# Negated scores, elu's negative part on ScalarE, and another order on VectorE in a graph attention kernel

## Chip, cores and metric

One core of a Trainium2 chip runs the whole program. The metric is device time in microseconds (us). The engines are TensorE (PE in the profile; PEld for its weight loads), VectorE (DVE), ScalarE (ACT), GpSimd (POOL) and SyncE (SP, which only issues DMAs here). Each engine runs its own instructions in order and waits on semaphores for the others.

## The reference

The input is x, 8 graphs of 1024 nodes with 256 features, and an integer adjacency matrix for each. A first attention layer is followed by three more, each with a feed-forward network, and by normalisations. The change touches the first layer only:

```python
h = jnp.einsum('bni,oi->bno', x, W) + b
ha = jnp.einsum('bmi,ij->bmj', h, attn)
scores = jnp.einsum('bmj,bnj->bmn', ha, h)
scores = jnp.where(adjacency_matrix == 0, -jnp.inf, scores)
attn_weights = jax.nn.softmax(scores, axis=-1)
x_out = jnp.einsum('bmn,bnd->bmd', attn_weights, h)
x = _layernorm(x + jax.nn.elu(x_out), axis=-1)
```

elu(z) is z where z is positive and exp(z) - 1 elsewhere.

## The kernel before

Matrix products run in float32r with every operand split in a high and a low part: ScalarE copies a PSUM result to the high part, VectorE subtracts that from PSUM to get the low part, and TensorE adds three products (high by high, low by high, high by low).

The first stage, `first_stage`, works on 64 tiles of 128 rows, 8 tiles for each of the 8 graphs (a batch here). The work is software-pipelined in 64 slots, one for each tile, and every engine's order in a slot is written out by hand in a function `emit(b, par, first, last)`; a slot is a turn of its loop over k. In slot k the engines work on tiles at different steps:

- PE: one projection of the next batch (`project`), the scores of tile k+2, in even slots a second projection, the transposes of tile k+1's probabilities into the PSUM tensor `PT`, and the product with the values of tile k (24 matmuls into the PSUM bank O).
- ACT: high parts of the projections (`proj_hi`), elu's exp of tile k-1 (`elu_exp`), the softmax's exp of tile k+2 (`softmax_exp`, with the negated row maximum as bias), high parts of the transposed probabilities of tile k+1.
- DVE: `scaled` (z of tile k-1: a reciprocal and z), `norm` of tile k-2, the low part of the first projection (`proj_lo`), `projections` of tile k-2 (two row sums), `negative_part` (min(z, 0)) of tile k-1, `mask0_tile` of tile k+3, `masked_scores` of tile k+2 (adds the mask, takes the row maximum, and a second small instruction negates it), in even slots the low part of the second projection, `residual_stats` of tile k-1 (z's positive part plus x, then plus elu's exp, then the statistics), `transposed_lo` of tile k+1, and what the next stage wants done beside it.
- POOL: `mask1_tile` of tile k+3 (two instructions that wait for `mask0_tile`), then 1/deviation of tile k-1, for which `norm` waits.

A batch has 12 projections, and `SLOT_OF = ((0, 1), (2,), (3, 4), (5,), (6, 7), (8,), (9, 10), (11,))` gives them to the 8 slots. Projections 0 to 3 transpose x, 4 to 7 make the keys (their low part, line 477, has a bias column), 8 to 11 the values. They share one PSUM bank J, so projection p waits until VectorE has made the low part of projection p-1. The last batch (slots 56 to 63) has no projections.

Beside this, `beside(slot)` of the next stage gives VectorE `raw_lo` (line 1697) at the end of slots 2, 4, ... 16 and `row_top` (line 1556) at the end of slots 24, 26, ... 38 and 42, 44, ... 56. At the end of slots 21, 31, 41, 43 and 59 TensorE transposes a few columns to a line (`v_line`, `r_line`) in `PT`, which ScalarE copies out; it first waits until VectorE has read the probabilities of tile slot+1 there: `pe.wait_ge(stage.s_tlo, 2 * (slot + 2))`.

After the first stage come 24 pairs of attention and feed-forward work (`graph_layers`), which the change leaves as they are.

Of the kernel before, what the change touches and what calls it, by code (L numbers as in the profile page):

```python
# [12 lines left out]
P = 128  # L13
F32 = mybir.dt.float32
# [3 lines left out]
ALU = mybir.AluOpType  # L18
ACT = mybir.ActivationFunctionType
# [100 lines left out]
def first_stage(nc, ctx, mem, x, adj, W, bias, attn, aw0, x1_dram, mask_dram, w1, s_next_x):  # L120
# [12 lines left out]
    def sb(name, shape, dt=F32, on="always"):  # L133
        return mem.place("a_" + name, shape, dt, on)

    def sem(name):
        return ctx.enter_context(nc.semaphore("a_" + name))
# [7 lines left out]
    shift_col = sb("shift_col", [P, KD])  # L145
    mx = sb("mx", [P, 2])
    nmx = sb("nmx", [P, 2])
    rinv = sb("rinv", [P, 2])
# [61 lines left out]
    s_t = sem("masked")  # L210
    s_nm = sem("max_negated")
    s_p = sem("probs")
# [148 lines left out]
    def scalar(act, beside):  # L361
# [8 lines left out]

        def fold_hi(step, to):

            act.wait_ge(s_fold, 2 * step + 1)
            act.activation(to[0][:, :, :], mem.A[:, step, :].rearrange("p (k d) -> p k d", d=D), ACT.Copy).then_inc(s_fhi, 1)

# [16 lines left out]
        def softmax_exp(b, k):  # L392
            act.wait_ge(s_nm, NT * b + k + 1)
            act.activation(t[k % 2][:, :], t[k % 2][:, :], ACT.Exp, bias=nmx[:, k % 2:k % 2 + 1]).then_inc(s_p, 1)

# [9 lines left out]
        def elu_exp(b, k):  # L405
            act.wait_ge(s_neg, NT * b + k + 1)
            act.activation(neg[:, k % 2, :], neg[:, k % 2, :], ACT.Exp).then_inc(s_ex, 1)

        fold_hi(0, awT)
        for p in range(2):  # L410
            proj_hi(0, 0, p)
        fold_hi(1, mid)
        for p in range(2, PJ):
# [5 lines left out]
        def emit(b, par, first, last):  # L419
            for k in range(NT):  # L420
                before = (b + (k - 1) // NT, (k - 1) % NT)
                if not last:
                    proj_hi(b + 1, 1 - par, SLOT_OF[k][0])
                if not (first and k == 0):
                    elu_exp(*before)
                if not last:
                    for p in SLOT_OF[k][1:]:
                        proj_hi(b + 1, 1 - par, p)
                if not (last and k + 2 >= NT):
                    softmax_exp(b + (k + 2) // NT, (k + 2) % NT)  # L430
                if not (last and k + 1 >= NT):
                    transposed_hi(b + (k + 1) // NT, (k + 1) % NT, first and k == 0)
                beside(NT * b + k)
# [5 lines left out]
    def vector(dve, beside):  # L439
# [14 lines left out]

        def fold_lo(step, to):

            dve.wait_ge(s_fhi, step + 1)
            dve.tensor_tensor(to[1][:, :, :], mem.A[:, step, :].rearrange("p (k d) -> p k d", d=D), to[0][:, :, :].bitcast(F32),
                              ALU.subtract).then_inc(s_flo, 1)

        def folded_column(step, to, done):

            pair = mem.A[:, 2, 2 * KD * step:2 * KD * (step + 1)].rearrange("p (k i) -> p k i", i=2)
            dve.wait_ge(s_fold, 2 * step + 2)
            dve.tensor_copy(to[:, :], pair[:, :, 0]).then_inc(s_bias, 1)
            dve.wait_ge(s_bias, done + 1)
            dve.tensor_tensor(to[:, :], pair[:, :, 1], to[:, :], ALU.add).then_inc(s_bias, 1)

# [15 lines left out]
        def mask0_tile(b, k, start):  # L484

            dve.wait_ge(s_adj[k % AR], 16 * (NT // AR * b + k // AR + 1))
            if not start:
                dve.wait_ge(s_t, NT * b + k - 1)
            dve.tensor_scalar(mask0[:, k % 2, :], adj_t[:, k % AR, :], 0.0, MASKED, ALU.is_equal, ALU.mult)\
               .then_inc(s_mask0, 1)  # L490

        def masked_scores(b, k, start):
            n = NT * b + k
            i = k % 2
            dve.wait_ge(s_mask0, n + 1)
            if start:
                wait_alone(dve, s_passed, (s_s, n + 1))
            else:
                wait_alone(dve, s_passed, (s_s, n + 1), (s_tr, 2 * (n - 1)))
            dve.tensor_tensor_reduce(out=t[i][:, :], in0=S[i][:, :], in1=mask0[:, i, :], scale=1.0, scalar=LOWEST,  # L500
                                     op0=ALU.add, op1=ALU.max, accum_out=mx[:, i:i + 1]).then_inc(s_t, 1)
            dve.wait_ge(s_t, n + 1)
            dve.tensor_scalar(nmx[:, i:i + 1], mx[:, i:i + 1], -1.0, None, ALU.mult).then_inc(s_nm, 1)

# [7 lines left out]
        def scaled(b, k):  # L512
            n = NT * b + k
            i = k % 2
            out = values_bank(b, k)
            dve.wait_ge(s_pv, n + 1)
            dve.reciprocal(rinv[:, i:i + 1], out[:, D:D + 1]).then_inc(s_rinv, 1)
            if n == 0:
                dve.wait_ge(s_brow, 16)
            else:  # L520
                dve.wait_ge(s_ln, LN * (n - 1) + 1)
            dve.wait_ge(s_rinv, n + 1)
            dve.scalar_tensor_tensor(z[:, :], out[:, 0:D], rinv[:, i:i + 1], bias_row[:, :], ALU.mult, ALU.add).then_inc(s_z, 1)

        def negative_part(b, k, start):
            n = NT * b + k
            dve.wait_ge(s_z, n + 1)
            if not start:
                dve.wait_ge(s_ln, LN * (n - 1) + 2)
            dve.tensor_scalar(neg[:, k % 2, :], z[:, :], 0.0, None, ALU.min).then_inc(s_neg, 1)  # L530

# [41 lines left out]

        fold_lo(0, awT)
        folded_column(0, through, 2)
        dve.wait_ge(s_bias, 4)
# [3 lines left out]
        for p in range(2):  # L580
            proj_lo(0, 0, p)
        fold_lo(1, mid)
        folded_column(1, shift_col, 6)
        for p in range(2, PJ):
# [8 lines left out]
        def emit(b, par, first, last):  # L593
            for k in range(NT):
                before = (b + (k - 1) // NT, (k - 1) % NT)
                if not (first and k == 0):
                    scaled(*before)
                if not (first and k <= 1):
                    norm(b + (k - 2) // NT, (k - 2) % NT, first and k <= 3)
                if not last:  # L600
                    proj_lo(b + 1, 1 - par, SLOT_OF[k][0])
                if not (first and k <= 1):
                    projections(b + (k - 2) // NT, (k - 2) % NT)
                if not (first and k == 0):
                    negative_part(*before, first and k == 1)
                if not (last and k + 3 >= NT):
                    mask0_tile(b + (k + 3) // NT, (k + 3) % NT, False)
                if not (last and k + 2 >= NT):
                    masked_scores(b + (k + 2) // NT, (k + 2) % NT, False)
                if not last:  # L610
                    for p in SLOT_OF[k][1:]:
                        proj_lo(b + 1, 1 - par, p)
                if not (first and k == 0):
                    residual_stats(before[0], par if k else 1 - par, before[1], first and k == 1)
                if not (last and k + 1 >= NT):
                    transposed_lo(b + (k + 1) // NT, (k + 1) % NT)
                beside(NT * b + k)

        batches(emit)
        scaled(B - 1, NT - 1)  # L620
        beside(NT * B)
        norm(B - 1, NT - 2, False)
        beside(NT * B + 1)
        projections(B - 1, NT - 2)
        beside(NT * B + 2)
        negative_part(B - 1, NT - 1, False)
        beside(NT * B + 3)
# [6 lines left out]
    def tensor(pe, beside, line_copied):  # L634
# [59 lines left out]
        def scores(b, par, j, start):  # L694
# [3 lines left out]
            if not start:  # L698
                pe.wait_ge(s_t, n - 1)
            ts = slice(j * P, (j + 1) * P)  # L700
            for c in range(NC):
# [6 lines left out]
        def transpose_probs(b, j, start):  # L708
            n = NT * b + j
            pe.wait_ge(s_p, n + 1)  # L710
            line_copied(n - 2)
            for g in range(2):
# [66 lines left out]
def layer_buffers(nc, ctx, mem, x, w1, s_rows):  # L779
# [17 lines left out]
    L.x = mem.x_rows  # L797
    L.A, L.G, L.Y, L.lines = mem.A, mem.G, mem.Y, mem.PT
    L.half = sb("half", [P, TC])
# [144 lines left out]
def graph_layers(nc, L, stage, x, rows, out, mask, turned, split, vline, rline, par):  # L944
# [26 lines left out]

    mask_rows = mask.rearrange("t p n -> (t p) n")

    def layer_of(k):
# [425 lines left out]
    def scalar(act):  # L1400
# [86 lines left out]
        def beside(slot):  # L1487
            if slot in SPLIT_AT:
                raw_hi(0, SPLIT_AT[slot])
            if slot in V_AT:  # L1490
                copy_v_line(V_AT[slot], L.lines[0:NT, 0:P])
            if slot in R_AT:
                copy_r_line(R_AT[slot], L.lines[0:2 * NT, 0:P])
            if slot == LAST + 3:
# [321 lines left out]
    def tensor(pe):  # L1816
# [99 lines left out]
        def beside(slot):  # L1916
            if slot in V_AT or slot in R_AT:
                pe.wait_ge(stage.s_tlo, 2 * (slot + 2))
            if slot in V_AT:
                v_line(V_AT[slot], L.lines[0:NT, 0:P])  # L1920
            if slot in R_AT:
                r_line(R_AT[slot], L.lines[0:2 * NT, 0:P])

# [107 lines left out]
```

## Time and profile before

| | |
|---|---|
| median of 3 runs | 2374.94 us (2374.61 to 2379.54) |
| the profiled execution | 2380.74 us |
| its span, first to last instruction | 2378.9 us |
| busy: PE, DVE, ACT, POOL | 2290.9, 2079.5, 1679.2, 1120.4 us |
| first stage, about | 0 to 595 us of the span |
| mean granted TensorE clock | 0.988 of full speed |

A timeline row gives the start of an instruction, its length in us, engine, source line, operation, the tile written and the tiles read, and, in brackets, how long the engine was idle before it and which instruction released it. VectorE overlaps the end of one instruction with the start of the next, so what an instruction costs is the time to the start of the next, a little less than its length.

### The profile page before, as it was taken

The numbers are of one execution on the slowest core, as the hardware profiler recorded it, in microseconds if no ns is written. First come the engines' busy times: TensorE is split into PE (matmuls) and PEld (weight loads), VectorE is DVE, ScalarE is ACT, GpSimd is POOL, SyncE is SP. The second block draws the span as 40 slices with busy tenths as digits, with TensorE's granted clock in tenths as the row PEclk, the third lists the DMA queues.
The fourth block names the chain that finished last, engine by engine and source line by source line (L and its number), as shares of the span: only waits on it lengthen the run. The fifth ranks groups of instructions, "written<-read, shape, count | busy, mean of one in ns | idle before, by whom it ended". The sixth has DMA issues, their size and how long they took to land. (4 is left out here: it accounts for less than half of the span.)

```text
span 2378.9 us, 44930 instructions
## 1 busy us (share of the span) xinstructions
PE 2290.9 (96%) x15996; PEld 2120.0 (89%) x15996; DVE 2079.5 (87%) x4848; ACT 1679.2 (71%) x2684; POOL 1120.4 (47%) x1315
## 2 busy tenths in 40 slices
PE   8999999997999999999999999999999999999996
PEld 7988888896998988999999999999999999899995
DVE  5998998999798988889979899899897998989875
ACT  3443433334788878888878888888887878878784
POOL 3555665664334442444434445434344555555531
PEclk9999999999999999999999999999999999999998
DMA  5665555467977778777665575665575656556431
GB/s 167 185 189 166 158 162 162 140 180 206 241 208 196 207 208 227 197 185 217 190 212 155 180 217 168 197 195 165 167 225 172 186 153 203 167 180 186 116 98 45
DMA packets 282800, 427.01 MB, mean 179 GB/s; under 512 B 89360, under 2 KB 183248, under 8 KB 282576
## 3 DMA queue, kind: packets, MB, share of 16 engines
q1 hardware_dynamic: 254928, 323.47, 43.8%
q0 software_dynamic: 27648, 100.68, 18.3%
q8 instruction: 126, 2.06, 0.3%
q14 instruction: 98, 0.80, 0.1%
HBM read 226.65 MB, written 79.99 MB: 129 GB/s over the span
## 5 line engine op out<-in xcount | busy, mean ns | idle before, releaser
L1861 PE MATMUL A<-x_hi,pT_hi 128*128 128x258 f32 x1536 | 437.0, 285 | 16.6 <-DVE pT_lo L1574 12.2
L1911 PE MATMUL Y<-w,g_hi 128*128 128x256 f32 x1536 | 438.4, 285 | 5.8 <-DVE g_lo L1665 4.7
L1862 PE MATMUL A<-x_hi,pT_lo 128*128 128x258 f32 x1536 | 434.1, 283 | 0.0
L1863 PE MATMUL A<-x_lo,pT_hi 128*128 128x256 f32 x1536 | 432.1, 281 | 0.0
L1912 PE MATMUL Y<-w,g_hi 128*128 128x256 f32 x1536 | 430.8, 280 | 0.0
L1913 PE MATMUL Y<-w,g_lo 128*128 128x256 f32 x1536 | 430.2, 280 | 0.0
L1476 ACT ACTIVATE g<-PT,b_less 128x512 f32<-128x512 f32 x384 | 263.7, 687 | 215.0 <-PE PT L47 210.3
L1339 POOL DMA_DIRECT2D t<-maskT x192 | 173.3, 951 | 418.6 <-DVE t L1567 399.0
L1665 DVE TENSOR_TENSOR g_lo<-g,g_hi 128x512 fp32r<-128x512 f32 x384 | 263.2, 685 | 79.2 <-ACT g_hi L1479 78.8
L1574 DVE TENSOR_TENSOR pT_lo<-t,pT_hi 128x512 fp32r<-128x512 f32 x384 | 255.6, 684 | 76.0 <-ACT t L1435 75.9
L45 PE MATMUL PT<-h_hi,w 128*128 128x512 f32 x768 | 308.3, 401 | 12.3 <-ACT g_hi L1479 9.1
L1911 PEld LDWEIGHTS Y<-w,g_hi 128*128 128x128 f32 x1536 | 289.7, 189 | 28.4 <-DVE g_lo L1665 11.8
L1861 PEld LDWEIGHTS A<-x_hi,pT_hi 128*128 128x128 f32 x1536 | 291.0, 189 | 24.0 <-issue 16.1
L47 PE MATMUL PT<-h_lo,w 128*128 128x512 f32 x768 | 304.2, 396 | 0.0
L46 PE MATMUL PT<-h_hi,w 128*128 128x512 f32 x768 | 303.2, 395 | 0.0
L1912 PEld LDWEIGHTS Y<-w,g_hi 128*128 128x128 f32 x1536 | 290.4, 189 | 10.0
L1913 PEld LDWEIGHTS Y<-w,g_lo 128*128 128x128 f32 x1536 | 292.2, 190 | 0.0
L1863 PEld LDWEIGHTS A<-x_lo,pT_hi 128*128 128x128 f32 x1536 | 291.1, 190 | 0.0
L1862 PEld LDWEIGHTS A<-x_hi,pT_lo 128*128 128x128 f32 x1536 | 290.3, 189 | 0.0
L1567 DVE SCALAR_TENSOR_TENSOR t<-rrow,v 128x512 f32<-128x512 f32 x384 | 280.4, 742 | 0.0
L1434 ACT ACTIVATE pT_hi<-t,v 128x512 fp32r<-128x512 f32 x384 | 272.8, 711 | 3.2 <-DMA t<-maskT 2.6
L1435 ACT ACTIVATE t<-t,v 128x512 f32<-128x512 f32 x384 | 271.8, 708 | 0.0
(189 smaller groups left out, 5843.1 us busy)
## 6 DMA issues: line engine op xcount, KB each, us to landing
t<-maskT POOLq DMA_DIRECT2D x192, 512.0 KB, 5.0
mask<-mask SPq DMA_DIRECT2D x192, 256.0 KB, 5.0
a_adj_t<-in_adj SPq DMA_DIRECT2D x64, 512.0 KB, 4.4
maskT<-turned SPq DMA_DIRECT2D x64, 512.0 KB, 5.1
rrow<-rline SPq DMA_DIRECT2D x96, 256.0 KB, 5.2
x_rows<-rows SPq DMA_DIRECT2D x24, 1024.0 KB, 8.1
mask<-a_mask SPq DMA_DIRECT2D x64, 256.0 KB, 4.7
turned<-maskT SPq DMA_DIRECT2D x32, 512.0 KB, 7.1
```

Of the source, the lines that this page charges most:

```text
L45: pe.matmul(out, left_hi, right_hi, start=start, stop=False)
L46: pe.matmul(out, left_lo, right_hi, start=False, stop=False)
L47: return pe.matmul(out, left_hi, right_lo, start=False, stop=stop)
L1434: act.activation(L.pT[0][:, n % P_RING, :], L.t[:, j, :], ACT.Exp, bias=bias).then_inc(L.s_exp, 1)
L1435: act.activation(L.t[:, j, :], L.t[:, j, :], ACT.Exp, bias=bias).then_inc(L.s_exp, 1)
L1567: dve.scalar_tensor_tensor(L.t[:, j, :], L.rrow[:, 0, k % 2, :], L.v8[:, k // 2 % VS, j:j + 1], L.rrow[:, 1, k % 2, :], ALU.add, ALU.max). ...
L1861: pe.matmul(L.A[:, t, 0:DE], hi, L.x_hi[par][:, j, :], start=(j == 0), stop=False)
L1862: pe.matmul(L.A[:, t, 0:DE], lo, L.x_hi[par][:, j, :], start=False, stop=False)
L1863: mm = pe.matmul(L.A[:, t, 0:D], hi, L.x_lo[par][:, j, :], start=False, stop=(j == NT - 1))
L1911: pe.matmul(L.Y[:, t, :], hi, w2_part(0, f), start=False, stop=False)
L1912: pe.matmul(L.Y[:, t, :], hi, w2_part(1, f), start=False, stop=False)
L1913: mm = pe.matmul(L.Y[:, t, :], lo, w2_part(0, f), start=False, stop=last and t % 2 == 1)
```

## The change

Four things change, all around the first stage.

1. The folded weights `mid` and the column `shift_col` get a factor of -1, so that the keys and the scores come out negated. The mask becomes +1e30, VectorE takes the least value of a row (`least`), and ScalarE's exp uses it as bias with scale -1. The instruction that negated the maximum goes, and ScalarE waits for `s_t` in place of `s_nm`.
2. min(z, 0) goes from VectorE. ScalarE computes max(-z, 0) itself and then exp of its negative: two instructions in place of one.
3. ScalarE does elu before the first projection of a slot. VectorE does `projections` one tile later (tile k-3) in `norm`'s place, and `norm` of tile k-2 after `masked_scores`.
4. TensorE's lines go to the first rows of a score bank that has been read, in place of `PT`, and the scores that come next in that bank wait for ScalarE's copy.

```diff
         def softmax_exp(b, k):
-            act.wait_ge(s_nm, NT * b + k + 1)
-            act.activation(t[k % 2][:, :], t[k % 2][:, :], ACT.Exp, bias=nmx[:, k % 2:k % 2 + 1]).then_inc(s_p, 1)
+            act.wait_ge(s_t, NT * b + k + 1)
+            act.activation(t[k % 2][:, :], t[k % 2][:, :], ACT.Exp, bias=least[:, k % 2:k % 2 + 1], scale=-1.0).then_inc(s_p, 1)
...
         def elu_exp(b, k):
-            act.wait_ge(s_neg, NT * b + k + 1)
-            act.activation(neg[:, k % 2, :], neg[:, k % 2, :], ACT.Exp).then_inc(s_ex, 1)
+            n = NT * b + k
+            act.wait_ge(s_z, n + 1)
+            if n >= 2:
+                act.wait_ge(s_ln, LN * (n - 2) + 2)
+            act.activation(neg[:, k % 2, :], z[:, :], ACT.Relu, scale=-1.0).then_inc(s_neg, 1)
+            act.wait_ge(s_neg, n + 1)
+            act.activation(neg[:, k % 2, :], neg[:, k % 2, :], ACT.Exp, scale=-1.0).then_inc(s_ex, 1)
...
                 before = (b + (k - 1) // NT, (k - 1) % NT)
-                if not last:
-                    proj_hi(b + 1, 1 - par, SLOT_OF[k][0])
                 if not (first and k == 0):
                     elu_exp(*before)
                 if not last:
+                    proj_hi(b + 1, 1 - par, SLOT_OF[k][0])
                     for p in SLOT_OF[k][1:]:
...
-            dve.tensor_tensor_reduce(out=t[i][:, :], in0=S[i][:, :], in1=mask0[:, i, :], scale=1.0, scalar=LOWEST,
-                                     op0=ALU.add, op1=ALU.max, accum_out=mx[:, i:i + 1]).then_inc(s_t, 1)
-            dve.wait_ge(s_t, n + 1)
-            dve.tensor_scalar(nmx[:, i:i + 1], mx[:, i:i + 1], -1.0, None, ALU.mult).then_inc(s_nm, 1)
+            dve.tensor_tensor_reduce(out=t[i][:, :], in0=S[i][:, :], in1=mask0[:, i, :], scale=1.0, scalar=-LOWEST,
+                                     op0=ALU.add, op1=ALU.min, accum_out=least[:, i:i + 1]).then_inc(s_t, 1)
...
                 if not (first and k == 0):
                     scaled(*before)
-                if not (first and k <= 1):
-                    norm(b + (k - 2) // NT, (k - 2) % NT, first and k <= 3)
+                if not (first and k <= 2):
+                    projections(b + (k - 3) // NT, (k - 3) % NT)
                 if not last:
                     proj_lo(b + 1, 1 - par, SLOT_OF[k][0])
-                if not (first and k <= 1):
-                    projections(b + (k - 2) // NT, (k - 2) % NT)
-                if not (first and k == 0):
-                    negative_part(*before, first and k == 1)
                 if not (last and k + 3 >= NT):
                     mask0_tile(b + (k + 3) // NT, (k + 3) % NT, False)
                 if not (last and k + 2 >= NT):
                     masked_scores(b + (k + 2) // NT, (k + 2) % NT, False)
+                if not (first and k <= 1):
+                    norm(b + (k - 2) // NT, (k - 2) % NT, first and k <= 3)
                 if not last:
                     for p in SLOT_OF[k][1:]:
                         proj_lo(b + 1, 1 - par, p)
...
+            line_copied(n - 3)
             ts = slice(j * P, (j + 1) * P)
...
+    def free_scores(slot, n):
+
+        return L.A[0:n, 2 * ((slot + 1) % 2), 0:P]
...
             if slot in V_AT or slot in R_AT:
-                pe.wait_ge(stage.s_tlo, 2 * (slot + 2))
+                pe.wait_ge(stage.s_t, slot + 2)
             if slot in V_AT:
-                v_line(V_AT[slot], L.lines[0:NT, 0:P])
+                v_line(V_AT[slot], free_scores(slot, NT))
```

## Rows read from the trace of the kernel before

**Rows 1.** Busy time in one batch: engines' us (x instructions), PEclk, DMA share, GB/s.

```profile
238.00:305.00 67.00, 65.08 (x440) 59.31 (x439) 63.21 (x163) 27.09 (x45) 42.00 (x37) 1.00 0.52 158
```

**Rows 2.** TensorE's waits from 100 to 700 us: total, times, longest us.

```profile
PE Y L45 <- DVE a_xT_lo L475: 8.6, 5, 2.2
```

**Rows 3.** Timeline of DVE: start us, us, instruction; first and last pairs' ends.

```profile
51.72 0.42 DVE L541 SCALAR_TENSOR_TENSOR a_y<-a_z,x_rows 128x256 f32<-128x256 f32 x1
...
512.72 0.82 DVE L541 SCALAR_TENSOR_TENSOR a_y<-a_z,x_rows 128x256 f32<-128x256 f32 x1
```

**Rows 4.** Timeline of DVE in slot 25, an odd one.

```profile
248.99 0.16 DVE L517 RECIPROCAL a_rinv<-Y 128x1 f32<-128x1 f32 x1
249.27 0.48 DVE L523 SCALAR_TENSOR_TENSOR a_z<-Y,a_rinv,a_bias_row 128x256 f32<-128x256 f32 x1
249.67 0.41 DVE L559 TENSOR_SCALAR a_xo<-a_y,a_mv,a_rstd 128x256 f32<-128x256 f32 x1
250.00 0.68 DVE L475 TENSOR_TENSOR a_xT_lo<-Y,a_xT_hi 128x512 fp32r<-128x512 f32 x1
250.60 0.41 DVE L571 SCALAR_TENSOR_TENSOR a_prod<-a_xo,a_aw 128x256 f32<-128x256 f32 x1
...
251.28 0.29 DVE L530 TENSOR_SCALAR a_neg<-a_z 128x256 f32<-128x256 f32 x1
251.49 0.69 DVE L489 TENSOR_SCALAR a_mask<-a_adj_t 128x1024 bf16<-128x1024 int32 x1
252.09 1.22 DVE L500 CUSTOM_DVE_ANT_0 a_t<-A,a_mask 128x1024 f32<-128x1024 f32 x1
...
253.46 0.79 DVE L541 SCALAR_TENSOR_TENSOR a_y<-a_z,x_rows 128x256 f32<-128x256 f32 x1
254.28 0.43 DVE L544 SCALAR_TENSOR_TENSOR a_y<-a_neg,a_y 128x256 f32<-128x256 f32 x1
```

**Rows 5.** Timeline of DVE in slot 26, an even one.

```profile
256.58 0.16 DVE L517 RECIPROCAL a_rinv<-Y 128x1 f32<-128x1 f32 x1
...
257.84 0.68 DVE L475 TENSOR_TENSOR a_xT_lo<-Y,a_xT_hi 128x512 fp32r<-128x512 f32 x1
...
259.33 0.68 DVE L489 TENSOR_SCALAR a_mask<-a_adj_t 128x1024 bf16<-128x1024 int32 x1
...
261.26 0.74 DVE L477 SCALAR_TENSOR_TENSOR a_yT_lo<-Y,a_shift_col,a_yT_hi 128x512 fp32r<-128x512 f32 x1
261.91 0.42 DVE L541 SCALAR_TENSOR_TENSOR a_y<-a_z,x_rows 128x256 f32<-128x256 f32 x1
...
264.67 1.21 DVE L1556 CUSTOM_DVE_ANT_0 spare<-vrow,mask 128x1024 bf16<-128x1024 f32 x1
...
265.81 0.16 DVE L517 RECIPROCAL a_rinv<-Y 128x1 f32<-128x1 f32 x1
```

**Rows 6.** Timeline of ACT in slots 24 and 25.

```profile
242.69 0.42 ACT L407 ACTIVATE a_neg<-a_neg 128x256 f32<-128x256 f32 x1 [2.52 <-DVE a_neg L530]
243.01 0.58 ACT L382 ACTIVATE a_xT_hi<-Y 128x512 fp32r<-128x512 f32 x1
...
251.60 0.42 ACT L407 ACTIVATE a_neg<-a_neg 128x256 f32<-128x256 f32 x1 [4.04 <-DVE a_neg L530]
```

**Rows 7.** Timeline of POOL in slot 25.

```profile
252.93 3.63 POOL L336 TENSOR_SCALAR a_mask<-a_adj_t 128x1024 bf16<-128x1024 int32 x1 [0.22 <-POOL a_adj_t L331]
```

**Rows 8.** Timeline of PE at two of its waits.

```profile
258.57 0.50 PE L45 MATMUL Y<-a_xT_hi,a_mid_hi 128*128 128x512 f32 x1 [1.92 <-DVE a_xT_lo L475]
...
391.29 0.38 PE L1825 MATMUL PT<-ident,rcol 128*16 128x128 f32 x1 [2.49 <-DVE a_pT_lo L509]
```

**Rows 9.** Busy time and granted clock in the microsecond after the second of them.

```profile
392.00:393.00 1.00, 1.00 (x5) 0.91 (x4) 0.41 (x1) 0.43 (x1) 0.06 (x1) 0.50 0.95 147
```

**Rows 10.** Groups of DVE by line: busy us, mean ns; idle us.

```profile
L1697 DVE TENSOR_TENSOR early<-early 128x512 fp32r<-128x512 f32 x8 | 5.5, 682 | 0.0
```

**Rows 11.** Timeline of DVE in slot 60, in the last batch.

```profile
555.07 1.23 DVE L500 CUSTOM_DVE_ANT_0 a_t<-A,a_mask 128x1024 f32<-128x1024 f32 x1 [1.80 <-issue]
```

More of the change, by code:

```diff
@@ L145, in first_stage @@
     shift_col = sb("shift_col", [P, KD])
-    mx = sb("mx", [P, 2])
-    nmx = sb("nmx", [P, 2])
+    least = sb("least", [P, 2])
     rinv = sb("rinv", [P, 2])
@@ L210, in first_stage @@
     s_t = sem("masked")
-    s_nm = sem("max_negated")
     s_p = sem("probs")
@@ L369, in scalar, with fold_hi @@
             act.activation(wT[0][:, k, :], PT[:, k * BANK:k * BANK + D], ACT.Copy).then_inc(s_whi, 1)
-        def fold_hi(step, to):
+        def fold_hi(step, to, sign):
             act.wait_ge(s_fold, 2 * step + 1)
-            act.activation(to[0][:, :, :], mem.A[:, step, :].rearrange("p (k d) -> p k d", d=D), ACT.Copy).then_inc(s_fhi, 1)
+            act.activation(to[0][:, :, :], mem.A[:, step, :].rearrange("p (k d) -> p k d", d=D), ACT.Copy,
+                           scale=sign).then_inc(s_fhi, 1)
         def proj_hi(b, par, p):
@@ L405, in elu_exp @@
         def elu_exp(b, k):
-            act.wait_ge(s_neg, NT * b + k + 1)
-            act.activation(neg[:, k % 2, :], neg[:, k % 2, :], ACT.Exp).then_inc(s_ex, 1)
-        fold_hi(0, awT)
+            n = NT * b + k
[5 more added lines that the diff above has]
+            act.activation(neg[:, k % 2, :], neg[:, k % 2, :], ACT.Exp, scale=-1.0).then_inc(s_ex, 1)
+        fold_hi(0, awT, 1.0)
         for p in range(2):
             proj_hi(0, 0, p)
-        fold_hi(1, mid)
+        fold_hi(1, mid, -1.0)
         for p in range(2, PJ):
@@ L453, in vector, with fold_lo, folded_column @@
                               ALU.subtract).then_inc(s_wlo, 1)
-        def fold_lo(step, to):
+        def fold_lo(step, to, sign):
             dve.wait_ge(s_fhi, step + 1)
-            dve.tensor_tensor(to[1][:, :, :], mem.A[:, step, :].rearrange("p (k d) -> p k d", d=D), to[0][:, :, :].bitcast(F32),
-                              ALU.subtract).then_inc(s_flo, 1)
-        def folded_column(step, to, done):
+            dve.scalar_tensor_tensor(to[1][:, :, :], mem.A[:, step, :].rearrange("p (k d) -> p k d", d=D), sign,
+                                     to[0][:, :, :].bitcast(F32), ALU.mult, ALU.subtract).then_inc(s_flo, 1)
+        def folded_column(step, to, done, sign):
             pair = mem.A[:, 2, 2 * KD * step:2 * KD * (step + 1)].rearrange("p (k i) -> p k i", i=2)
             dve.wait_ge(s_fold, 2 * step + 2)
-            dve.tensor_copy(to[:, :], pair[:, :, 0]).then_inc(s_bias, 1)
+            dve.tensor_scalar(to[:, :], pair[:, :, 0], sign, None, ALU.mult).then_inc(s_bias, 1)
             dve.wait_ge(s_bias, done + 1)
-            dve.tensor_tensor(to[:, :], pair[:, :, 1], to[:, :], ALU.add).then_inc(s_bias, 1)
+            dve.scalar_tensor_tensor(to[:, :], pair[:, :, 1], sign, to[:, :], ALU.mult, ALU.add).then_inc(s_bias, 1)
         def proj_lo(b, par, p):
@@ L488, in mask0_tile @@
                 dve.wait_ge(s_t, NT * b + k - 1)
-            dve.tensor_scalar(mask0[:, k % 2, :], adj_t[:, k % AR, :], 0.0, MASKED, ALU.is_equal, ALU.mult)\
+            dve.tensor_scalar(mask0[:, k % 2, :], adj_t[:, k % AR, :], 0.0, -MASKED, ALU.is_equal, ALU.mult)\
                .then_inc(s_mask0, 1)
@@ L521, in scaled @@
                 dve.wait_ge(s_ln, LN * (n - 1) + 1)
+                dve.wait_ge(s_neg, n)
             dve.wait_ge(s_rinv, n + 1)
             dve.scalar_tensor_tensor(z[:, :], out[:, 0:D], rinv[:, i:i + 1], bias_row[:, :], ALU.mult, ALU.add).then_inc(s_z, 1)
[L525 to L530, printed above, removed]
         def residual_stats(b, par, k, start):
@@ L572, in projections @@
                                          accum_out=uv[:, NC * b + k // TC, j, k % TC:k % TC + 1]).then_inc(s_uv, 1)
-        fold_lo(0, awT)
-        folded_column(0, through, 2)
+        fold_lo(0, awT, 1.0)
+        folded_column(0, through, 2, 1.0)
         dve.wait_ge(s_bias, 4)
@@ L581, in vector @@
             proj_lo(0, 0, p)
-        fold_lo(1, mid)
-        folded_column(1, shift_col, 6)
+        fold_lo(1, mid, -1.0)
+        folded_column(1, shift_col, 6, -1.0)
         for p in range(2, PJ):
@@ L621, in vector @@
         beside(NT * B)
+        projections(B - 1, NT - 3)
         norm(B - 1, NT - 2, False)
@@ L625, in vector @@
         beside(NT * B + 2)
-        negative_part(B - 1, NT - 1, False)
         beside(NT * B + 3)
@@ L710, in transpose_probs @@
             pe.wait_ge(s_p, n + 1)
-            line_copied(n - 2)
             for g in range(2):
@@ L797, in layer_buffers @@
     L.x = mem.x_rows
-    L.A, L.G, L.Y, L.lines = mem.A, mem.G, mem.Y, mem.PT
+    L.A, L.G, L.Y = mem.A, mem.G, mem.Y
     L.half = sb("half", [P, TC])
@@ L1490, in beside @@
             if slot in V_AT:
-                copy_v_line(V_AT[slot], L.lines[0:NT, 0:P])
+                copy_v_line(V_AT[slot], free_scores(slot, NT))
             if slot in R_AT:
-                copy_r_line(R_AT[slot], L.lines[0:2 * NT, 0:P])
+                copy_r_line(R_AT[slot], free_scores(slot, 2 * NT))
             if slot == LAST + 3:
@@ L1917, in beside @@
             if slot in V_AT or slot in R_AT:
-                pe.wait_ge(stage.s_tlo, 2 * (slot + 2))
+                pe.wait_ge(stage.s_t, slot + 2)
             if slot in V_AT:
-                v_line(V_AT[slot], L.lines[0:NT, 0:P])
+                v_line(V_AT[slot], free_scores(slot, NT))
             if slot in R_AT:
-                r_line(R_AT[slot], L.lines[0:2 * NT, 0:P])
+                r_line(R_AT[slot], free_scores(slot, 2 * NT))
         def rest():
```

## The prediction

> **What bounds the kernel now.** I read the busy shares in slices first: the change lies in the first stage, the first quarter of the span, where PE and DVE are both above 90%. The busy time of one batch says how close they are: in 67.0 us TensorE is idle 1.92 us, so 8 tiles cost it 65.1 us, 16.3 us a pair of slots, at full clock [rows 1]. The waits come next: TensorE's largest is one kind, once a batch, at the second projection of slots 2 modulo 8, where the first key product waits for VectorE's low part of x [rows 2, 8]. VectorE has no such wait: its timeline is a chain in which each instruction starts before the last has quite ended. An odd slot takes it 256.58 - 248.99 = 7.59 us [rows 4]. An even one takes 264.67 - 256.58 = 8.09 us, and 1.14 us more with a `row_top` [rows 5]. A pair is 15.68 us without, 16.82 us with it, against TensorE's 16.3. So VectorE sets the pace from slot 24 on, with TensorE a few per cent behind it; before slot 24 they are about even (`raw_lo`, 8 times, adds some 0.60 us [rows 10]). From tile 0's first residual step to tile 54's, 27 odd and 27 even slots, the stage takes 512.72 - 51.72 = 461.0 us [rows 3]. VectorE's bare work in it is 27 x 15.68 + 8 x 0.60 + 15 x 1.14 = 445.3 us; the other 15.7 us are waits on ScalarE and TensorE.
>
> **VectorE sheds work.** In an odd slot `negative_part` costs 0.21 us (to the next start). The negated maximum lies between 252.09 and 253.46, 1.37 us for `masked_scores` with it against 1.14 us for the instruction of the same kind in `row_top`, so 0.23 us goes [rows 4, 5]. `norm` leaves the place ahead of the projection, 0.33 us there. In even slots the same place also held a wait for POOL (z to the low part takes 257.84 - 256.58 - 0.28 = 0.98 us there against 0.73 us in the odd slot [rows 4, 5]), and that goes too.
>
> **A round trip comes in.** After the change ScalarE does elu ahead of the slot's first projection, and elu starts from z, which VectorE makes at the head of the same slot. The low part of that projection is VectorE's fifth instruction, and all behind it waits. With the slot's start at 0: z starts at 0.28 and ends at 0.76 [rows 4]. ScalarE takes over 0.03 us after a VectorE end (251.28 + 0.29 to 251.60 [rows 4, 6]): 0.79. The relu is not in the trace; the nearest row is the exp of the same tile, 0.42 us; below it stands VectorE's min of it at 0.29, above it an eviction of twice the columns at 0.58 [rows 4, 6]. I take 0.42, as the row has the same engine, tile and size: 1.21. The exp waits for it (0.03 again): 1.24. The projection's high part starts 0.32 us after an exp starts and lasts 0.58 [rows 6]: it ends at 2.14, and VectorE can begin its low part at about 2.18. In the meantime it has only the two row sums (0.28 + 0.40 + 0.68): it is free at 1.36. So it stands still for 0.82 us in every slot of the first seven batches. Before, the first high part stood ahead of elu in ScalarE's order and was done before VectorE came to it: in the rows its low part follows without idle time [rows 4, 5]. With 0.60 us for the low part (0.65 for a key's, 2 of 8, and its high part longer: 0.04 on average) the mask begins at 2.82 us, against 2.50 before in the odd slot and 2.75 in the even one [rows 4, 5].
>
> By the Trainium skill, "ScalarE: Activation LUTs", section "Rules for kernel authors", relu belongs on VectorE rather than ScalarE; it speaks against the move for the length of the instruction. By its formula (186 ns and 0.833 ns an element) the relu would be 0.40 us, an estimate, and the slot 0.02 us shorter; the exp's row agrees, and what costs here is the place in the order.
>
> **norm's new place.** After the mask comes POOL's `mask1_tile`, whose long instruction starts 1.44 us after the mask's start (251.49 to 252.93 [rows 4, 7]). VectorE's `masked_scores` and low parts, which read PSUM, run through it at their usual length (261.26: 0.74 [rows 5]). The residual step of the odd slot, with all operands in SBUF, does not: it lasts 0.79 instead of 0.42 us and ends 1.32 us after POOL's start, so that it really ran from 0.90 us after it [rows 4, 5, 7]. In even slots it comes later and is not held. `norm` now comes at 0.60 + 1.14 + 0.04 = 1.78 us after the mask, inside that time, and all its operands are in SBUF too. The trace has no `norm` there. Bounds: not held, and it starts at 1.78; held to the end of the row, 1.44 + 1.32 = 2.76. I take the row's own release, 1.44 + 0.90 = 2.34, since the nearest row is that residual step: same engine, same size, SBUF to SBUF. With 0.33 us for `norm` the next may start at 2.67.
>
> The Trainium skill, "SBUF — State Buffer", section "SBUF: two separate sides", says that VectorE and GpSimd share a pair of ports under an exclusive lock, and that a VectorE instruction in a two-port mode, or with two SBUF inputs, waits for the whole GpSimd instruction. The row agrees that it waits and not that it waits for the whole: 0.90 of 3.63 us. By the page norm would start 2.73 us later still, 147 us over 54 slots (an estimate), which the row's 0.90 gives no chance.
>
> **The sum.** Odd slot: 2.82 + 2.67 + 0.45 (residual step) + 2.30 (254.28 to 256.58) = 8.24 us, 0.65 more. Even slot: 2.82 + 2.67 + 0.65 (second low part) + 2.76 (261.91 to 264.67) = 8.90 us, 0.81 more [rows 4, 5]. The second high part does not come last: its low part can start 2.47 us or so after the first low part's end, at 5.3, and is wanted at 5.49. A pair is 17.14 us, above TensorE's 16.3, so VectorE sets the pace in every batch: 27 x 17.14 + 4.8 + 17.1 = 484.7 us against 461.0, +23.7 us. TensorE's waits for lines in these batches go, but they are then hidden behind VectorE.
>
> The last batch has no projection and so no round trip. Its slots lose 0.21, 0.33 and 0.23 us (and a wait) and get 0.33 to 0.56 us back at `norm`: some 0.3 us shorter in five slots and 0.4 in three, 2.7 us. The line of slot 59 no longer waits for VectorE; the 1.80 us for which `masked_scores` then stood still goes [rows 11]. Together 4.5 us; I count 4, as the start of the next stage also waits for DMAs.
>
> TensorE's clock: after a wait of 2.49 us it was granted half its speed, 1.2 instead of 2.4 GHz; after one of 1.92 us it stayed [rows 1, 8, 9]. The wait for the low part of x grows by 0.9 us or more, as that part ends 2.86 us into the slot and no longer 1.94 (257.84 + 0.68 [rows 5]). So the clock may fall once a batch; then the key product comes a microsecond later to VectorE. I take +3 us, between 0 and 8.
>
> ScalarE and POOL have room, and SP's store of x1, now 4 us later in its slot, comes before SP's next mask wait as it did. These are 0. Total: 23.7 - 4 + 3 = +23 us on the profiled run's 2380.7, 2403.7; that run stood 5.8 us above the median, so 2398 us.
>
> **Rivals.** A: norm is not held. Then the odd slot is 2.82 + 2.79 + 2.30 = 7.91, the even one 2.82 + 2.11 + 0.65 + 2.76 = 8.34 and up to 0.4 more for the second high part, a pair 16.55, 468.7 us: +7.7, less 4, 2379 us. For it: instructions with a PSUM operand pass freely there. Against: norm has none.
>
> B, faster: TensorE is the bound. If ScalarE's path from z to the high part is hidden, VectorE needs under 16.3 us a pair, and the stage falls to what TensorE needs: the 15.7 us of waits go and 4 at the end, 2355 us. It decides from the point where VectorE's stand is under 0.4 us a slot. For it: TensorE is 97% busy. Against: the path of 1.9 us from z has 1.1 us of cover, all by rows.
>
> C: longer holds, to 2.76 in every slot (0.42 x 54 = 22.7 us), or the clock falling in all batches and VectorE waiting on the way back: 2412 to 2421 us. Against: both ends of the hold are seen in one row.
>
> D: the lines don't do what they say, as the next scores wait for ScalarE's copy at the end of its slot: five times a microsecond at most, and no longer on the path; within the forecast.
>
> **How the numbers follow.** Forecast 0.61 (its own range 2388 to 2410), A with D 0.17, B 0.16, C 0.06. The measurement tells 0.2% (4.7 us) from no change. A is slower by that in 4 of 10, faster in 1 of 10 or so. Slower 0.61 + 0.06 + 0.06 = 0.73, less 0.01 for what I have missed, 0.72; same 0.10; faster 0.18. The range from 2370 to 2411 leaves out most of B and C.
>
> **What would show it.** Right: in the changed profile VectorE's low parts (xT, yT, hn) idle about 0.8 us for ScalarE in nearly every slot, norm's row near 0.9 us instead of 0.41 in slots with a mask, pairs of slots at 17 to 18 us, TensorE waiting longer for the low part of x. Wrong: those waits under 0.4 us and TensorE without waits (B), or norm at 0.41 (A).

## The result and the profile after

The changed kernel takes 2401.09 us (median of 4 runs, 2395.36 to 2408.97) against 2376.41 us before in runs beside it (4 runs). The ratio is 1.0105, with a 95% interval of 1.0071 to 1.0138: slower, by 24.7 us between the medians, where 2398 us had been forecast. The profiled execution took 2408.97 us, its span 2407.2 us.

The time went where the forecast put it, into the first stage. This is VectorE in slot 25 of the changed kernel, the slot of [rows 4] (start us, us, instruction, idle before and releaser); low parts are now lines 478, 480 and 484, norm is line 554, the residual step line 536:

```profile
260.97 0.16 DVE L518 RECIPROCAL a_rinv<-Y 128x1 f32<-128x1 f32 x1
261.27 0.48 DVE L525 SCALAR_TENSOR_TENSOR a_z<-Y,a_rinv,a_bias_row 128x256 f32<-128x256 f32 x1
261.67 0.41 DVE L566 SCALAR_TENSOR_TENSOR a_prod<-a_xo,a_aw 128x256 f32<-128x256 f32 x1
...
263.17 0.69 DVE L478 TENSOR_TENSOR a_xT_lo<-Y,a_xT_hi 128x512 fp32r<-128x512 f32 x1 [0.73 <-ACT a_xT_hi L381]
263.78 0.68 DVE L492 TENSOR_SCALAR a_mask<-a_adj_t 128x1024 bf16<-128x1024 int32 x1
264.38 1.22 DVE L503 CUSTOM_DVE_ANT_0 a_t<-A,a_mask 128x1024 f32<-128x1024 f32 x1
...
265.52 0.89 DVE L554 TENSOR_SCALAR a_xo<-a_y,a_mv,a_rstd 128x256 f32<-128x256 f32 x1
266.50 0.43 DVE L536 SCALAR_TENSOR_TENSOR a_y<-a_z,x_rows 128x256 f32<-128x256 f32 x1
...
269.26 0.16 DVE L518 RECIPROCAL a_rinv<-Y 128x1 f32<-128x1 f32 x1
```

The slot takes 269.26 - 260.97 = 8.29 us, against 7.59 before. Two things in it are new. After the two row sums VectorE stands still for 0.73 us until ScalarE has the high part. And norm lasts 0.89 us where it lasted 0.41. ScalarE in the same slot shows the round trip, z (ends 261.75), relu, exp, high part, without a gap:

```profile
261.79 0.42 ACT L409 ACTIVATE a_neg<-a_z 128x256 f32<-128x256 f32 x1 [3.87 <-DVE a_z L525]
262.24 0.42 ACT L411 ACTIVATE a_neg<-a_neg 128x256 f32<-128x256 f32 x1
262.56 0.58 ACT L381 ACTIVATE a_xT_hi<-Y 128x512 fp32r<-128x512 f32 x1
```

POOL's mask instruction began 0.29 us before norm was issued:

```profile
265.23 3.63 POOL L334 TENSOR_SCALAR a_mask<-a_adj_t 128x1024 bf16<-128x1024 int32 x1 [0.22 <-POOL a_adj_t L329]
```

Norm ended at 266.41, 1.18 us after POOL's start, so with its own 0.41 us it ran from 0.77 us after it.

All of VectorE's waits for high parts from 40 to 600 us (total, times, longest us) come to 47.9 us. In the kernel before they were 10.7 us; these are its three lines, then those of the changed kernel:

```profile
DVE a_yT_lo L477 <- ACT a_yT_hi L386: 5.4, 10, 1.3
DVE a_hn_lo L481 <- ACT a_hn_hi L389: 4.4, 9, 1.1
DVE a_xT_lo L475 <- ACT a_xT_hi L382: 0.9, 2, 0.7
```

```profile
DVE a_yT_lo L480 <- ACT a_yT_hi L385: 16.5, 19, 1.2
DVE a_xT_lo L478 <- ACT a_xT_hi L381: 16.0, 20, 1.4
DVE a_hn_lo L484 <- ACT a_hn_hi L388: 15.4, 21, 0.7
```

TensorE's waits from 100 to 700 us, where [rows 2] had 8.6 us in five:

```profile
PE Y L45 <- DVE a_xT_lo L478: 18.0, 6, 3.6
PE Y L667 <- DVE a_xT_lo L478: 7.2, 6, 1.6
...
PE A L45 <- ACT line L1409: 4.0, 2, 3.1
```

The longest come in slots 2 modulo 8, as before. After the one in slot 26 the clock was granted at half (PE timeline, then the busy times of one microsecond with PEclk as the third number from the end), and VectorE then waited for the second high part too:

```profile
272.21 0.72 PE L45 MATMUL Y<-a_xT_hi,a_mid_hi 128*128 128x512 f32 x1 [3.58 <-DVE a_xT_lo L478]
```

```profile
273.00:274.00 1.00, 1.00 (x3) 0.72 (x3) 1.00 (x3) 0.00 (x0) 0.78 (x2) 0.50 1.06 365
```

```profile
275.82 0.75 DVE L480 SCALAR_TENSOR_TENSOR a_yT_lo<-Y,a_shift_col,a_yT_hi 128x512 fp32r<-128x512 f32 x1 [1.13 <-ACT a_yT_hi L385]
```

From tile 0's residual step to tile 54's the stage takes 490.4 us, against 461.0 in [rows 3]. The residual step of the last tile starts 24.0 us later than before (611.37 against 587.40). The rest of the program took 4 us more in this execution, which is within what single executions differ by.

```profile
51.68 1.09 DVE L536 SCALAR_TENSOR_TENSOR a_y<-a_z,x_rows 128x256 f32<-128x256 f32 x1
...
542.12 0.43 DVE L536 SCALAR_TENSOR_TENSOR a_y<-a_z,x_rows 128x256 f32<-128x256 f32 x1
```

### The profile page after: what moved, and what is told of

Its sections match the earlier page's. It is cut to its first block and busy times, and to the rows that moved or that the text cites. A ratio compares the mean times of both kernels' runs of the same rounds, so it can differ in the third digit from the quotient of the medians.

```text
span 2407.2 us, 44869 instructions
## 1 busy us (share of the span) xinstructions
PE 2303.6 (96%) x15996; PEld 2126.4 (88%) x15996; DVE 2073.4 (86%) x4720; ACT 1699.5 (71%) x2748; POOL 1105.5 (46%) x1315
## 5 line engine op out<-in xcount | busy, mean ns | idle before, releaser
L1858 PEld LDWEIGHTS A<-x_hi,pT_hi 128*128 128x128 f32 x1536 | 292.2, 190 | 27.9 <-issue 16.3
```

Source lines behind the costliest of these rows:

```text
L1858: pe.matmul(L.A[:, t, 0:DE], hi, L.x_hi[par][:, j, :], start=(j == 0), stop=False)
```

## The experiments

The theory had two mechanisms, the round trip over ScalarE and the hold of norm behind POOL. The rivals: that the relu on ScalarE is what costs; that TensorE's clock is; that TensorE or ScalarE comes last in any case. All ratios are to the kernel before in runs on the same chip, with 95% intervals. "The stage" is the time from tile 0's residual step to tile 54's in the profiled execution.

**The projection ahead of elu again.** In the changed kernel:

```diff
+                if not last:
+                    proj_hi(b + 1, 1 - par, SLOT_OF[k][0])
                 if not (first and k == 0):
                     elu_exp(*before)
                 if not last:
-                    proj_hi(b + 1, 1 - par, SLOT_OF[k][0])
```

> The changed kernel with one thing undone: ScalarE does the slot's first projection ahead of elu again. Theory (the round trip z, relu, exp, projection holds VectorE 0.82 us a slot): VectorE's idle time for ScalarE's high parts falls from 48 us in the changed kernel to under 12 us, an odd slot to 1.96 + 2.67 + 0.45 + 2.30 = 7.4 us and an even one to about 8.0, a pair to 15.4, which is under TensorE's 16.3, so TensorE sets the pace: 2360 to 2370 us. norm is still held (0.9 us). Rival, relu on ScalarE itself is what costs (ScalarE's softmax and transposes come later): stays above 2390 us. Rival, TensorE's clock falls cause the loss: the falls would have to go by themselves; 2390 or more if they stay.

Measured: ratio 0.9970 (0.9951 to 0.9989), median 2368.97 us against 2378.02; the stage 454.1 us, 36.4 less than in the changed kernel. VectorE's waits from 40 to 600 us:

```profile
DVE a_t L504 <- issue: 19.9, 31, 1.0
...
DVE a_yT_lo L481 <- ACT a_yT_hi L385: 3.9, 10, 0.6
DVE a_hn_lo L485 <- ACT a_hn_hi L388: 2.9, 8, 0.4
DVE a_xT_lo L479 <- ACT a_xT_hi L381: 0.2, 1, 0.2
```

Those for high parts fell from 47.9 to 7.0 us; what VectorE waits for now is mostly TensorE's scores (line 504). The profile names no releaser there ("issue"), but the one in slot 27 starts at 267.43, 0.17 us after the last score product of its tile (266.87 + 0.39). So the place of two lines on ScalarE makes this change slower, and without it the change is faster than before. The relu is still on ScalarE, so that rival falls. The clock followed by itself: in slots 2 modulo 8 up to slot 50 it fell to half five times in the changed kernel (from 129, 201, 273, 348 and 491 us) and once here (from 257 us). So these falls come with the round trip; what they added to the loss by themselves was not tried.

**norm ahead of the mask.** In the changed kernel, on VectorE:

```diff
                 if not (first and k <= 2):
                     projections(b + (k - 3) // NT, (k - 3) % NT)
+                if not (first and k <= 1):
+                    norm(b + (k - 2) // NT, (k - 2) % NT, first and k <= 3)
...
-                if not (first and k <= 1):
-                    norm(b + (k - 2) // NT, (k - 2) % NT, first and k <= 3)
```

> The changed kernel with one thing undone: norm goes ahead of the mask again, behind the two row sums and ahead of the first low part, where VectorE stands still. Theory (norm is held behind POOL's mask until 0.90 us after its start): norm's length is 0.41 us in all slots, the residual step of odd slots is held again (0.8 us); odd slots 7.9 us, even ones 8.0 to 8.7, a pair about 16.6; VectorE still idles for ScalarE, some 0.5 us a slot instead of 0.8; about 2385 us, 9 over before. Rival, the hold costs nothing because TensorE or ScalarE comes last anyway: the same time as the changed kernel, 2400 us.

Measured: ratio 1.0046 (1.0029 to 1.0062), median 2388.42 us; the stage 472.5 us, 18.0 less. The durations of norm and of the residual step (ns, least/median/most):

```profile
L554 DVE TENSOR_SCALAR a_xo<-a_y,a_mv,a_rstd x64: 405/408/427, 55.0 to 596.7; 128x256 f32<-128x256 f32 x64
...
L536 DVE SCALAR_TENSOR_TENSOR a_y<-a_z,x_rows x64: 411/426/1302, 50.7 to 593.2; 128x256 f32<-128x256 f32 x64
```

Norm is at 0.41 us everywhere, and the residual step is held again: it lasts 1.01 or 1.02 us in most odd slots, once 1.30, where 0.8 was expected. The time is near the expected 2385 us. The second mechanism counts, and less than the first. This edit does not take the hold away; it moves it back to the residual step of the odd slots.

**Both undone.** The two edits above together.

> The changed kernel with both undone: projection ahead of elu on ScalarE, norm ahead of the mask on VectorE. What stays of the change: negated scores, the relu on ScalarE, lines in free score banks. Theory: VectorE needs about 7.4 us in odd and 7.5 to 8.2 in even slots, TensorE's 16.3 us a pair is the bound; faster than before by 8 to 18 us, 2358 to 2368 us. Rival, relu on ScalarE or the lines cost something by themselves: at 2375 or above.

Measured: ratio 0.9946 (0.9928 to 0.9965), median 2365.06 us; the stage 450.4 us. What is left of the change is a gain of some 13 us. The two mechanisms do not add up (36.4 + 18.0 against 40.1). That fits TensorE as the bound once the round trip is gone: from 60 to 500 us it is busy for 409.1 of 440 us in the changed kernel, for 431.3 with the projection ahead again and for 433.5 here.

**POOL's mask on half of the columns.** In the changed kernel:

```diff
-            pool.tensor_scalar(mask1[:, i, :], adj_t[:, a, :], 0.0, MASKED, ALU.is_le, ALU.mult).then_inc(s_mask, 1)
+            pool.tensor_scalar(mask1[:, i, 0:N // 2], adj_t[:, a, 0:N // 2], 0.0, MASKED, ALU.is_le, ALU.mult).then_inc(s_mask, 1)
```

Two lines that the cut leaves out set the other half to zero once. This kernel so leaves half of that mask out, and its result is another one; it serves for the timing alone.

> The changed kernel with POOL's long mask instruction on half of the columns (the other half of that mask is left out, so the next layers see another mask). Theory (POOL holds norm): norm's hold shrinks or goes; if the hold is the instruction's first part in proportion, norm waits until about 0.45 us after its start, so 0.1 us, and lasts 0.5 us or less instead of 0.88: about 0.4 us less a slot, some 15 to 20 us faster than the changed kernel. If the hold is a fixed time after the start, norm stays at 0.88 and the time at 2400. Rival, norm's length comes from something else on VectorE (its two pointer operands, the order of writes): norm stays at 0.88 as well, even where the instruction starts later or is over.

Measured: ratio 1.0032 (1.0012 to 1.0051), median 2385.96 us; the stage 474.3 us. By the two ratios (1.0105 and 1.0032) that is 17 us under the changed kernel, as expected. POOL's instruction and norm in one slot:

```profile
281.49 1.93 POOL L335 TENSOR_SCALAR a_mask<-a_adj_t 128x512 bf16<-128x512 int32 x1 [0.22 <-POOL a_adj_t L330]
```

```profile
281.79 0.46 DVE L555 TENSOR_SCALAR a_xo<-a_y,a_mv,a_rstd 128x256 f32<-128x256 f32 x1
```

Nothing in norm or ahead of it on VectorE was changed, and it lasts 0.46 us (median of all too). It ended at 282.25, so it ran from 0.35 us after POOL's start, where it was 0.77 with all columns. So POOL's instruction holds it, and the hold goes with the size of the instruction.

Norms that were issued late say the same. In the changed kernel one was issued 0.68 us after POOL's start, not 0.30; it lasted only 0.50 us and again ended 1.18 us after that start. Those issued 0.80 us after it or later took 0.41 us. With half of the columns, those issued 0.35 us after it or later took 0.41 us too.

```profile
212.57 3.63 POOL L334 TENSOR_SCALAR a_mask<-a_adj_t 128x1024 bf16<-128x1024 int32 x1 [0.22 <-POOL a_adj_t L329]
```

```profile
213.25 0.50 DVE L554 TENSOR_SCALAR a_xo<-a_y,a_mv,a_rstd 128x256 f32<-128x256 f32 x1
```

**The odd slot's low part after the scores.** In the changed kernel, with ScalarE's order as changed, on VectorE:

```diff
-                if not last:
+                if not last and k % 2 == 0:
                     proj_lo(b + 1, 1 - par, SLOT_OF[k][0])
...
                     masked_scores(b + (k + 2) // NT, (k + 2) % NT, False)
+                if not last and k % 2 == 1:
+                    proj_lo(b + 1, 1 - par, SLOT_OF[k][0])
```

> The changed kernel, ScalarE's order as changed (elu ahead of the projection), but in odd slots VectorE makes the low part only after the masked scores, so that mask and scores cover ScalarE's round trip. Theory: in odd slots VectorE's idle time for ScalarE goes, and norm, 0.60 us later, is no longer held (0.41 us): an odd slot takes about 6.8 us, an even one 8.9 as before, a pair 15.7, under TensorE's 16.3; near 2378 us, 20 under the changed kernel. Rival, the order on ScalarE itself is what costs, whoever waits: stays at 2395 or above.

Measured: ratio 1.0061 (1.0038 to 1.0085), median 2392.03 us; the stage 476.8 us. This missed: 9 us under the changed kernel's median and not 20 (13.6 us in the stage). VectorE in an odd slot and at the next slot's low part:

```profile
275.31 0.17 DVE L518 RECIPROCAL a_rinv<-Y 128x1 f32<-128x1 f32 x1
...
278.06 1.22 DVE L503 CUSTOM_DVE_ANT_0 a_t<-A,a_mask 128x1024 f32<-128x1024 f32 x1 [0.67 <-issue]
...
279.88 0.41 DVE L554 TENSOR_SCALAR a_xo<-a_y,a_mv,a_rstd 128x256 f32<-128x256 f32 x1
...
283.09 0.16 DVE L518 RECIPROCAL a_rinv<-Y 128x1 f32<-128x1 f32 x1
...
285.39 0.75 DVE L480 SCALAR_TENSOR_TENSOR a_yT_lo<-Y,a_shift_col,a_yT_hi 128x512 fp32r<-128x512 f32 x1 [0.83 <-ACT a_yT_hi L385]
```

The odd slot did what was expected of VectorE: no wait for a high part, norm at 0.41. But it takes 7.78 us and not 6.8. Of that, 0.67 us is `masked_scores` standing still for TensorE's scores; the profile names no releaser, but the last score product of that tile ended at 277.89:

```profile
277.50 0.39 PE L47 MATMUL A<-a_xT_lo,a_yT_hi 128*128 128x512 f32 x1
```

And TensorE still waits in even slots, which were left as they were, for VectorE's low part:

```profile
PE Y L45 <- DVE a_xT_lo L478: 11.3, 6, 2.3
PE Y L669 <- DVE a_xT_lo L478: 7.0, 6, 1.7
```

So the round trip in even slots seems to cost twice, on VectorE and then on TensorE, whose second projection waits for that low part, and cover in odd slots alone gives VectorE time that TensorE cannot use. This reading is argued from the waits: no run covered the round trip in even slots alone or in both.

**The parts by themselves.** Each is the kernel before with one part of the change: the lines (`pe.wait_ge(stage.s_t, slot + 2)` and `free_scores` as in the change), elu's relu on ScalarE behind the projection (`negative_part` gone), and the negated scores (`least` for `mx` and `nmx`).

> The kernel before with only the lines changed (TensorE writes them to the free score bank). Theory: TensorE's waits at lines 1820 and 1825 (11.8 us in the kernel before) go, but VectorE sets the pace, so only the 1.8 us of slot 59 and a part of the rest come back: 2370 to 2375 us. Rival, the lines were on the path: 11 us or more faster, 2364 us or less. Rival, the next scores' wait for ScalarE's copy takes their place: 2375 or above, with waits of 1 to 3 us at the first score product after a line.

> The kernel before with only elu's negative part moved: ScalarE does relu and exp (behind the slot's first projection, as before), VectorE has no negative_part. Theory: VectorE loses 0.21 us ahead of the mask in every slot, 0.42 us of a pair of 16.8, so that TensorE's 16.3 us a pair comes close; 5 to 10 us faster than before, 2367 to 2372 us. Rival (Trainium skill, ScalarE: Activation LUTs, Rules for kernel authors: relu is for VectorE): no gain or slower, 2377 or more, since ScalarE's 0.42 us is longer than VectorE's 0.29.

> The kernel before with only the scores negated (the instruction that negates the row maximum goes). Theory: in even slots VectorE is 0.2 us shorter; in odd slots nothing, as the residual step then waits for POOL's hold until the same moment (it lasts longer, 1.0 us instead of 0.8, and the next step starts 2.79 us after the mask as before): 27 x 0.2 = 5 us of VectorE at most, 2 to 5 us of the time, 2372 to 2375 us. Rival, it counts in every slot: 10 us or more, 2367 or less.

Measured: the lines 0.9983 (0.9971 to 0.9995), the relu 0.9985 (0.9968 to 1.0002), the negated scores 0.9992 (0.9975 to 1.0008). The first is a gain, some 4 us, as expected; the other two cannot be told from nothing. The relu's forecast of 5 to 10 us was on the high side (4.5 us by the medians, 2371.37 against 2375.89; the interval allows for up to 7.6), and moving it to ScalarE does no harm. With the lines moved, TensorE still waits, for ScalarE's copy (total, times, longest us):

```profile
PE A L45 <- ACT line L1416: 4.3, 2, 3.1
```

The negated scores show why they give little: in odd slots the residual step, issued earlier, only lasts longer, and the next step (line 541) starts 2.80 us after the mask, as in [rows 4] (2.79):

```profile
285.07 0.69 DVE L488 TENSOR_SCALAR a_mask<-a_adj_t 128x1024 bf16<-128x1024 int32 x1
...
286.82 1.01 DVE L538 SCALAR_TENSOR_TENSOR a_y<-a_z,x_rows 128x256 f32<-128x256 f32 x1
287.87 0.42 DVE L541 SCALAR_TENSOR_TENSOR a_y<-a_neg,a_y 128x256 f32<-128x256 f32 x1
```

**Two further versions.** Both undone, and besides the odd slot's low part after the scores, as above; then the same with the last line at slot 61 in place of 59, where TensorE waits for ScalarE's copy of it before the next stage's products.

> Projection ahead of elu on ScalarE, norm ahead of the mask, and in odd slots the low part after the masked scores, so that the residual step comes after POOL's hold. Theory: odd slots need 6.8 us of VectorE, pairs 14.6 to 15; TensorE's 16.3 us a pair bounds all batches; 2 to 6 us under the kernel with both undone: 2356 to 2363 us, TensorE's waits for VectorE under 5 us in the full batches. Rival, nothing more to gain since TensorE sets the pace there already: the same as with both undone, 2365 us.

> The kernel of the same call with the late low part, and the last line moved from slot 59 to slot 61, where no scores follow in its bank. Theory: the 3 us for which TensorE's scores wait for ScalarE's copy of the line go; 2 to 3 us faster than that kernel if TensorE's place there is on the path. Rival: hidden behind VectorE in the last batch, no difference.

Measured: 0.9937 (0.9917 to 0.9957), median 2363.16 us, the stage 448.5 us; and with the line moved 0.9950 (0.9929 to 0.9971), 2365.14 us. Both beat the kernel before and the changed one. Neither can be told from the version with both undone (0.9946, 0.9928 to 0.9965), so the runs don't decide whether the first gained the 2 us or so that it may have gained. TensorE has little left to gain there: it is busy for 435.7 of the 440 us from 60 to 500 us. With the line moved, TensorE's wait of 3.0 us for the copy turned into one at the transposes in the same place:

```profile
PE PT L713 <- DVE a_pT_lo L511: 3.0, 1, 3.0
```

That fits VectorE setting the pace of the last batch, so that it does not matter for what TensorE waits there.

## Why the prediction was right

- The round trip: right in mechanism and size. An idle time of 0.82 us a slot was worked out; 0.73 us for transposes and values and 0.83 for keys were seen. Relu and exp each took 0.42 us, as the nearest row had. Undoing it took 32 us off by the two ratios to before (1.0105 and 0.9970 of 2376 to 2378 us).
- norm held by POOL: right, shown by the half mask. The release was taken from the residual step at 0.90 us after POOL's start; for norm it was 0.77. In odd slots that gained nothing, as the residual step started 0.09 us after norm's end where an overlap of 0.08 had been counted: most odd slots took 8.24 to 8.40 us (8.24 worked out). In even slots a low part follows norm and did overlap with it; most that saw no fall of the clock took 8.7 or 8.9 us (8.90 worked out). In slots without a clock fall a pair with `row_top` takes 18.10 us (294.98 to 313.08, tile 27's residual step to tile 29's); 17.14 + 1.14 = 18.28 had been worked out.
- TensorE's clock: right in kind, undersized. With pairs of 18.10 us (16.96 without the 1.14 of `row_top`) the stage would be 27 x 16.96 + 4.8 + 17.1 = 479.8 us; it is 490.4. Of the 10.6 us between, 8.1 lie in the seven pairs with slots 2 modulo 8 (266.50 to 286.01, tile 24's residual step to tile 26's, 19.51 us, in the batch shown), where 3 us had been taken, 8 at most. There the sentence that the second high part does not come last failed: 1.13 us in the row above. In five of the seven the clock fell, after waits of 3.0 to 3.6 us, and these pairs exceed what they should take by 0.9 to 1.7 us. Of the two without a fall, the first of the stage exceeds it by 0.9 us and the one of slot 42 by 0.2. How the excess divides between the clock and the wait itself was not tried.
- The last batch gave 5.4 us back (29.4 less 24.0), where 4 were taken.
- The sum: 23.7 - 4 + 3 = 22.7 us worked out to the end of the stage, 24.0 seen. That it came so close is in part luck, as the terms were off against one another: TensorE's clock and waits by +7.6 (10.6 where 3 were taken, beyond the bound of 8), the slots by -4.9 (18.8 where 23.7 were worked out), the last batch by -1.4.
- Rival B named its point rightly: VectorE's stand under 0.4 us a slot. With the projection ahead of elu it is under that, TensorE sets the pace, and the kernel is faster; the forecast of 2355 us was lower than any version reached (2363). Rival D was a little off in size: TensorE waited 0.93 and 3.11 us for ScalarE's copies in the changed kernel (4.0 us together, above), the latter in the last batch.

By the Trainium skill, "SBUF — State Buffer", section "SBUF: two separate sides", a VectorE instruction in a two-port mode, or with two SBUF inputs, waits for the whole of POOL's instruction. The runs agree with the lock and not with its length: the residual step, with two SBUF inputs, waited for 0.90 of 3.63 us, norm for 0.77 of 3.63 with all columns and for 0.35 of 1.93 with half.

## What to carry to other kernels

Before an instruction is put ahead of another on an engine, ask what it waits for and who waits for the one behind it: here 0.84 us of ScalarE work, with room on ScalarE, cost 32 us because it put the head of VectorE's own slot between VectorE and its next instruction. Work taken off an engine pays only up to the next engine's need (TensorE's 16.3 us a pair); a round trip that the engine stands still for is paid for the most part (41 us of waiting for high parts, 32 us of time). When an instruction has all operands in SBUF, place it away from the start of a long GpSimd instruction: norm ran at 0.41 us ahead of the mask and at 0.88 behind it. One that reads PSUM ran there at its usual length (the key's low part at 0.74 us [rows 5]), but that putting it there makes the kernel faster was not shown (0.9937 against 0.9946).

## What the hardware showed that was not expected

- GpSimd's 1024-column instruction holds an SBUF-to-SBUF instruction of VectorE for its first 0.77 to 0.90 us of 3.63, and for 0.35 us of 1.93 with 512 columns: the hold goes with the size and ends long before the instruction does.
- Negating the row maximum cost VectorE 0.23 us in an odd slot, but where a hold follows, taking it away gives nothing: the held instruction starts earlier and ends at the same moment.
- A longer wait on TensorE was paid twice: 3.58 us of waiting, and a clock of half speed in the microseconds behind it. The length of one wait does not decide by itself: in the kernel before the clock fell after waits of 2.23 and 2.49 us and stayed after one of 2.63 us (at 573.35).
